# Each store of a conv tile as two transfers of 64 partitions on one queue

## What is computed

```python
g = relu(bn2(einsum('nchw,oc->nohw', x, wg1))).mean(axis=(2, 3))
xg0 = (relu(tanh(g @ wg2.T + bg2)) + beta)[0]              # of image 0 alone
param = ...                                                # xg0 cut into 32 groups of channels
filt = ...                                                 # each group gets one 7 x 7 DCT basis
xp = x.reshape(n, c, 7, 8, 7, 8).mean(axis=(3, 5))
y = relu(bn1(sum(xp * filt, axis=(2, 3)) @ w1d[:, :, 1].T + b1d))
x = x * y[:, :, None, None] + x
```

```python
t = relu(bn(x.mean(axis=(2, 3)) @ w1.T))
wt = (t @ w2.T + b2).reshape(b * 96, 1, 3, 3) * mask
out = conv(x, wt, padding=1, groups=b * 96) + bias
```

## Time and profile before

| | |
|---|---|
| median of two runs | 217.89 us (216.58 and 219.20) |
| span of the profiled execution, first to last instruction | 216.9 us |
| TensorE, VectorE, GpSimd, ScalarE busy | 96%, 88%, 80%, 62% of the span |
| mean granted TensorE clock | 0.978 |
| read from and written to memory | 40.48 MB, 38.54 MB |
| DMA queue of SP | 8352 packets, 78.91 MB |

### The profile page before, as it was taken

How to read it: one execution, slowest core, us unless ns; L and a number is a source line. 1 busy time by engine, 2 the same in 40 slices (tenths; PEclk the granted TensorE clock), 3 DMA queues, 4 the chain that set the end, 5 groups by cost and what they waited for, 6 DMA issues and landing times.

```text
span 216.9 us, 2648 instructions
## 1 busy us (share of the span) xinstructions
PE 207.2 (96%) x814; PEld 126.3 (58%) x814; DVE 190.0 (88%) x224; ACT 135.3 (62%) x208; POOL 172.9 (80%) x168
## 2 busy tenths in 40 slices
PE   7999989999999999999999999999999999999990
PEld 3458564475666566656655764675556656665550
DVE  4238679887999999999999999999999999889991
ACT  2020015568585768576857687677657796989960
POOL 0222049999999999999999999999999996887880
PEclk9999976999999999999999999999999999999997
DMA  5999999859999999999999999999999475627777
GB/s 154 360 424 429 431 422 427 372 178 326 386 417 390 400 420 421 424 435 423 423 435 428 426 419 430 428 426 431 423 426 396 192 298 222 262 111 296 296 304 290
DMA packets 8526, 79.18 MB, mean 365 GB/s; under 512 B 1056, under 2 KB 1440, under 8 KB 2496
## 3 DMA queue, kind: packets, MB, share of 16 engines
q1 hardware_dynamic: 8352, 78.91, 88.4%
q10 hardware_dynamic: 160, 0.10, 0.2%
HBM read 40.48 MB, written 38.54 MB: 364 GB/s over the span
## 4 chain that ended last, share of the span: by engine, by line
PE 54%; DVE 27%; DMA 9%; ACT 3%; SPq 3%; issue 2%; ACTq 0%; DVEq 0%
PE banks L913 43%; DVE banks L668 12%; DMA xin<-x 9%; DVE xout L668 5%; DVE xout L677 4%; PE banks L898 2%; ACT banks L748 2%; PE banks L842 2%; PE banks L905 2%; PE banks L884 2%; PE banks L886 2%; DVE stats L556 1%; DVE sums L575 1%; SPq L363 1%; DVE stats L572 1%
## 5 line engine op out<-in xcount | busy, mean ns | idle before, releaser
L913 PE MATMUL banks<-xin,diag 128*128 128x495 f32 (+4 forms) x480 | 159.1, 483 | 0.3 <-ACT banks L748 0.2
L913 PEld LDWEIGHTS banks<-xin,diag 128*128 128x128 f32 x480 | 88.5, 191 | 54.7 <-issue 39.0
L748 ACT ACTIVATE banks<-xin,wide_sb,coef 128x616 f32<-128x616 f32 (+5 forms) x77 | 84.8, 1120 | 20.1 <-DVE xout L677 9.4
L417 POOL TENSOR_TENSOR halves<-xin 128x1568 f32<-128x1568 f32 (+1 forms) x22 | 73.7, 3348 | 20.1 <-DMA xin<-x 20.0
L668 DVE SCALAR_TENSOR_TENSOR banks<-xin,coef,banks 128x1485 f32<-128x1485 f32 (+2 forms) x48 | 82.0, 1707 | 2.2 <-ACT banks L748 1.2
L668 DVE SCALAR_TENSOR_TENSOR xout<-xin,coef,banks 128x1485 f32<-128x1485 f32 (+5 forms) x31 | 41.6, 1362 | 0.6
L422 POOL TENSOR_TENSOR halves<-halves 128x784 f32<-128x784 f32 x18 | 33.3, 1850 | 1.4
L677 DVE SCALAR_TENSOR_TENSOR xout<-xin,coef,banks 128x990 f32<-128x990 f32 (+2 forms) x24 | 29.2, 1215 | 4.0 <-PE banks L913 3.8
L744 ACT ACTIVATE diag<-wide_sb,coef 128x128 f32<-128x128 f32 x72 | 23.4, 389 | 6.7 <-DVE coef L602 6.7
L789 ACT ACTIVATE xout<-banks 128x616 f32<-128x616 f32 (+3 forms) x24 | 16.0, 667 | 15.8 <-PE banks L913 15.3
L427 POOL TENSOR_TENSOR rows<-halves 128x392 f32<-128x392 f32 x18 | 18.3, 1019 | 1.4
(11 more groups left out here) (83 smaller groups left out, 133.9 us busy)
## 6 DMA issues: line engine op xcount, KB each, us to landing
xin<-x SPq DMA_DIRECT2D x23, 1568.0 KB, 10.3
out<-xout SPq DMA_DIRECT2D x23, 1568.0 KB, 12.5
xout<-x SPq DMA_DIRECT2D x3, 392.0 KB, 4.5
xin<-x SPq DMA_DIRECT2D x1, 1120.0 KB, 15.6
out<-xout SPq DMA_DIRECT2D x1, 616.0 KB, 3.3
out<-xout SPq DMA_DIRECT2D x1, 476.0 KB, 3.9
xin<-x SPq DMA_DIRECT2D x1, 448.0 KB, 16.2
wide_sb<-wide SPq DMA_DIRECT2D x1, 435.5 KB, 16.6
```

The costliest lines, as they stand in the source:

```text
L417: eng.tensor_tensor(halves[:, j % 2, first:end, :], cells[:, :, 0, :], cells[:, :, 1, :], ALU.add).then_inc(once_folded, 1)
L748: return sca.activation(acc, above_rows(k, first, end), ACT.Identity, bias=bias[:, k % PER:k % PER + 1], scale=weight(k, UP))
L913: return mm(to, diag[:, k % 2, which, :], grid(k)[:, irows, cols], start=False, stop=(which == LEFT), skip_group_check=True)
```

## The change

A store is issued as two transfers, of partitions 0 to 63 and of partitions 64 to 127, one right behind the other on SP's queue. Each of them raises the buffer's semaphore by 16, so every count that is waited for is doubled. Nothing else is changed: the same rows go to the same places, in the same order of tiles.

```diff
             def store(k, first=0, end=H):
-                sp.dma_start(out_tiles[k // PER, k % PER][:, first * W:end * W],
-                             xout[:, k % OUT_BUFS, first * W:end * W]).then_inc(stored[k % OUT_BUFS], 16)
+                for half in (slice(0, P // 2), slice(P // 2, P)):
+                    sp.dma_start(out_tiles[k // PER, k % PER][half, first * W:end * W],
+                                 xout[half, k % OUT_BUFS, first * W:end * W]).then_inc(stored[k % OUT_BUFS], 16)
...
-                sp.wait_ge(stored[b], 16 * (TILES // OUT_BUFS + parts))
+                sp.wait_ge(stored[b], 2 * 16 * (TILES // OUT_BUFS + parts))
...
-                    pool.wait_ge(stored[k % OUT_BUFS], 16 * (k // OUT_BUFS))
+                    pool.wait_ge(stored[k % OUT_BUFS], 2 * 16 * (k // OUT_BUFS))
```

More of the change, by code:

```diff
@@ L664, in tap @@
                     if k >= OUT_BUFS:
-                        dve.wait_ge(stored[k % OUT_BUFS], 16 * (k // OUT_BUFS))
+                        dve.wait_ge(stored[k % OUT_BUFS], 2 * 16 * (k // OUT_BUFS))
                 acc = acc_d(k, first, end).rearrange("p (r c) -> p r c", c=W)[:, :, ocols]
@@ L775, in part @@
                 n = k - (TILES - AHEAD_FOLD)
-                act.wait_ge(stored[k % OUT_BUFS], 16 * (k // OUT_BUFS))
+                act.wait_ge(stored[k % OUT_BUFS], 2 * 16 * (k // OUT_BUFS))
                 seed(k, xout[:, k % OUT_BUFS, top_p(k) * W:], top_p(k), H).then_inc(part_seeded, 1)
```

## The result

The changed kernel took 220.48 and 221.65 us, median 221.06, against 217.89 before: a ratio of 1.0207, with a 95% interval of 1.0122 to 1.0293. It is slower by some 2%, not by the 30% that was forecast. The interval lies wholly above 1, but on both sides of 1.02.

A forecast was written before the change was run, and what follows sets the result against it. DMA engines and TensorE were taken to bound the middle together; with halves the DMA queue throughout: 45.1 + 168.75 + 67.5 + 1.35 = 282.7 us, plus 1.0 gives 283.7 us. Likeliest case's range 265 to 292, whole range 216 to 292.

The forecast's parts named there:

- the sum at the upper bound: Whole DMA queue from 45.1 us: each load with halved store takes 11.25 us, last nine stores 7.5 each; 283.7 us, 51%.
- The price of a half-range transfer: Each half of a store: 3.75 us in the engines at 214 GB/s, plus 1.35 us fixed when alone.
- the rows that leaned to this bound: Small transfers on ScalarE's queue: 66 KB per us on 32 partitions against 95 on 128, above the fixed 1.35 us.
- half-way: Rival for stores: engines sharing partitions partly miss each other, half the extra is saved, 5.63 us a store; 238.8 us, 17%.
- the balance in the middle: From 66 to 156 us, a tile's load and store hold the DMA engines 7.5 us, exactly its period on TensorE.
- the 5 us of slack: Loads land about 5 us before GpSimd folds the tile, so that much backlog growth from 45 to 151 us is free.
- all sixteen engines take part in a narrow transfer: Each half of a store lies on all sixteen DMA engines, four rows on each instead of eight.
- SP's issues: 27 more transfers on SP, 0.42 us each at the median, cost nothing while SP waits 95.8 us for VectorE.
- the halves' landing: Late stores of 1568 KB: both halves land about 9 us after the first issue, not 5.1.
- SP at the end: Last four stores become eight, so the final half is issued later: bounds 0 and 0.9 us, taken 0.4.
- no change: Rival for stores: each engine paces its own rows, so halves cost 0 to 0.4 us; 218.0 us, 27%.
- the fixed part: Rival for the queue: a store's second half waits for the first's 1.35 us, load and store take 8.85; 226.1 us, 5%.

The follow-up runs named there:

- the three-way cut: Each store issued as three transfers (partitions 32 to 95, 0 to 31, 96 to 127) instead of the changed kernel's two halves; ratio 1.0443 to the kernel before.

## Why the prediction was wrong

**The step that failed** is the sum at the upper bound, in the words "So the queue never empties: 15 x 11.25 = 168.75". The price of a half-range transfer was nearly right where it stands alone: 5.6 us measured against 5.1 by my bound, though the rows that leaned to this bound proved little. The error was to carry it into a full queue. There the middle moved 401 to 427 GB/s with halves, not 285, and the 3.75 us for each of 15 stores, 56 us, came out as 4.2 us in all, the last load's lateness. 3.5 of them were there at the first load behind a halved store. I named that mechanism as the rival "half-way" but priced it at half the extra, for no reason except that it lay between; in the traces nearly all of it was won back. What the traces show directly is the rate. That each engine pulls ahead of the one with which it shares its way in, and the two then meet no more, is my reading of it; the uneven finish above supports it, and no row names single engines. Nor is such lateness a mark of half ranges alone, since the kernel with half of the image rows in each transfer had it too (14.3 us).

**Right:** the balance in the middle, with the DMA engines as full as TensorE, and the 5 us of slack. The last load was 4.2 us later, within the 5 that were free, and compute did not wait; in the three-way cut, with 8.2 us a tile, it did. Right, too, that all sixteen engines take part in a narrow transfer, that SP's issues cost nothing in the middle (though the two issues of a store together held SP for 1.3 to 3.8 us there: its waits for VectorE fell from 95.8 us to 67.2 and took that up), and that the halves' landing would be near 9 us after the first issue in the late stores (9.2).

**Missed:** SP at the end. The prediction bounded the cost of its issues at 0.9 us; measured, the last part's issue came 5.5 us after the end of compute, some 4 of them because slow halves held SP. Missed too: the last nine stores. I had given them no sum of their own, since the queue was to be full to the end. In fact they start on a queue that is nearly empty, once for each tile, so they run at 228 to 246 GB/s every time. That is still nearly enough for a tile in 6.2 us (1.606 MB / 0.235 = 6.8 us), so the backlog at the end is small: the 5.2 us between compute's end and the span's. The measured 221.06 us lies inside the whole range of 216 to 292 only because that range was stretched down to the rival "no change", and it is no success of the mechanism. The rivals "no change" and "the fixed part" fell, the one by the late part, the other by the kernels with half of the image rows and with every other partition in each transfer.

**Open:** why stores in halves recover and loads do not; why the kernel with half of the image rows in each transfer loads so late; and why the three-way cut stays at 390 GB/s in a full queue although its 64-partition transfer is a fast one.

## What to carry to other kernels

If a store must be cut, cut it by every other partition, which cost nothing here, or by its free dimension, which cost 0.2 to 1.1%, but not at partition 64: a transfer within 0 to 63 moves 201 GB/s alone (64 to 127 lands as late), against 401 from 32 to 95 and 437 over all partitions. A busy queue can hide this, so read a transfer's price where it stands: GB/s divided by the DMA share, stretch by stretch, showed at once 417 in the middle (421 / 1.01) and 240 at the end (228 / 0.95). Look at the part of the kernel where the queue runs empty before the end, since there a slow transfer goes straight into the time, also by holding the engine that issues the next ones.

## What the runs showed of the hardware that was not expected

- A train of stores in half ranges, alone in the queue, goes from 232 to 414 GB/s in some 16 us; loads in half ranges stayed at 216 to 221 GB/s for almost 40 us.
- 64 partitions from 32 to 95, or every other one, are nearly as fast as 128 (3.7 and 3.6 us for 784 KB, against 3.3), and 32 partitions from 0 take 3.3 us for 392 KB, against 2.4 over 128.
- With halves in a full queue the sixteen engines did not finish together: 6 us with a DMA share of 0.23 at the end of the kernel with added loads and halves.
- In a slow queue an issue holds SP longer: up to 2.3 us for one half of a part of the last tile, against 0.33 to 0.58 us for a whole part before.
